# Gated cross-attention with a routed feed-forward: ScalarE issues the copy of the negated maxima itself, in place of SyncE

## What is computed

```python
def _L0_xattn_ref(q, k, v, mask, Wq, bq, Wk, bk, Wv, bv):
    Qh = (q @ Wq + bq).reshape(B, S, H, dh)      # H = 16 heads, dh = 16
    Kh = (k @ Wk + bk).reshape(B, S, H, dh)
    Vh = (v @ Wv + bv).reshape(B, S, H, dh)
    scores = jnp.einsum('bqhd,bkhd->bhqk', Qh, Kh) / jnp.sqrt(jnp.float32(10.0))
    scores = jnp.where(mask[:, None, None, :] == 0, jnp.float32(-1000000000.0), scores)
    probs = jax.nn.softmax(scores, axis=-1)
    return jnp.einsum('bhqk,bkhd->bqhd', probs, Vh).reshape(B, S, D)
...
x = x + jnp.tanh(g_xattn[0]) * _L0_xattn_ref(_layernorm(x), ctx_1024, ctx_1024, mask, ...)
x = x + jnp.tanh(g_ffn[0]) * _L0_ffn_ref(_layernorm(x), ...)   # 8 experts, each takes its top 1024 tokens
```

## Time and profile before

| | us |
|---|---|
| time before, median of 3 | 867.7 |
| the profiled execution: its own time | 866.8 |
| its span | 865.1 |
| PE busy | 757.8 |
| DVE busy | 556.9 |
| ACT busy | 512.0 |
| mean granted clock of TensorE, share of full | 0.947 |

### The profile page before, as it was taken

How to read it: one execution, slowest core, us unless ns; L and a number is a source line. 1 busy time by engine, 2 the same in 40 slices (tenths; PEclk the granted TensorE clock), 3 DMA queues, 4 the chain that set the end, 5 groups by cost and what they waited for, 6 DMA issues and landing times. The chain is left out here.

```text
span 865.1 us, 24848 instructions
## 1 busy us (share of the span) xinstructions
PE 757.8 (88%) x9570; PEld 634.3 (73%) x9570; DVE 556.9 (64%) x1421; ACT 512.0 (59%) x1004; POOL 375.3 (43%) x793
## 2 busy tenths in 40 slices
PE   1699999999999999999998721599999999999993
PEld 1577788878887888878886510379888888888983
DVE  4367777787777777777767549754746556474440
ACT  3235577766766677767756637265555655556641
POOL 6231444534354344424422430436474654747505
PEclk9889999999999999999999955599999999999997
DMA  4423342444434452444322242135354453624314
GB/s 133 136 89 127 131 156 98 152 157 163 146 122 151 154 178 88 160 162 164 103 102 72 83 138 83 48 126 118 99 104 117 81 113 73 130 45 85 38 13 49
DMA packets 76772, 97.06 MB, mean 112 GB/s; under 512 B 8264, under 2 KB 55880, under 8 KB 76616
## 3 DMA queue, kind: packets, MB, share of 16 engines
q1 hardware_dynamic: 64368, 78.44, 26.7%
q0 software_dynamic: 12288, 17.05, 12.0%
HBM read 52.37 MB, written 25.72 MB: 90 GB/s over the span
## 5 line engine op out<-in xcount | busy, mean ns | idle before, releaser
L676 DVE TENSOR_REDUCE m_sb<-a_ps 128x4 f32<-128x512 f32 x256 | 164.5, 684 | 70.7 <-PE a_ps L905 60.1
L538 ACT ACTIVATE p_t<-b_ps 128x512 f32<-128x512 f32 x256 | 143.6, 588 | 61.1 <-PE b_ps L913 60.9
L905 PE MATMUL a_ps<-k_st,q_st 31*128 31x128 f32 x2048 | 151.0, 285 | 21.6 <-ACT p_t L538 11.4
L905 PEld LDWEIGHTS a_ps<-k_st,q_st 31*128 31x128 f32 x2048 | 127.2, 188 | 47.7 <-issue 37.0
L913 PE MATMUL b_ps<-q_st,k_st 32*128 32x128 f32 x2048 | 149.1, 283 | 1.2 <-ACT p_t L538 1.0
L1223 POOL DMA_INDIRECT out<-y,idx_add x64 | 100.3, 1567 | 110.8 <-ACT y L1282 100.0
L458 POOL TENSOR_TENSOR x<-o_n,x_res 128x256 f32<-128x256 f32 x64 | 47.0, 734 | 194.9 <-DVE o_n L761 171.6
L913 PEld LDWEIGHTS b_ps<-q_st,k_st 32*128 32x128 f32 x2048 | 124.5, 186 | 2.2 <-issue 1.4
L1592 PE MATMUL bank<-x_hi,w_hi 128*128 128x512 f32 x254 | 100.1, 394 | 0.0
L1592 PE MATMUL bank<-x_lo,w_hi 128*128 128x512 f32 x254 | 99.0, 390 | 0.0
L1592 PE MATMUL bank<-x_hi,w_lo 128*128 128x512 f32 x254 | 98.9, 389 | 0.0
(11 more groups left out here) (238 smaller groups left out, 1713.9 us busy)
## 6 DMA issues: line engine op xcount, KB each, us to landing
w<-in_w_t SPq DMA_DIRECT2D x24, 512.0 KB, 4.8
rows_scratch<-xg SPq DMA_DIRECT2D x16, 528.0 KB, 3.0
x_in<-in_x SPq DMA_DIRECT2D x16, 512.0 KB, 4.9
c_t<-in_ctx_t SPq DMA_DIRECT2D x16, 512.0 KB, 5.8
k_st<-k_val SPq DMA_DIRECT2D x64, 128.0 KB
q_st<-q_val SPq DMA_DIRECT2D x64, 128.0 KB, 2.1
x_res<-in_x SPq DMA_DIRECT2D x16, 512.0 KB, 3.8
out<-x SPq DMA_DIRECT2D x16, 512.0 KB, 6.4
```

What stands on the lines that cost most here:

```text
L538: act.activation(p_t[b.s % 2][:, 4 * r:4 * r + 4, :], b_ps[q % 2][:].rearrange("p (h s) -> p h s", s=P), ACT.Exp, scale=SCALE).then_inc(ex ...
L676: dve.tensor_reduce(m_sb[b.s % 2][:, 4 * q:4 * q + 4], a_ps[q % 2][:].rearrange("p (h s) -> p h s", s=P), AX_X, ALU.max).then_inc(max_done, 1)
L905: mm = pe.matmul(a_ps[i][:, t * P:(t + 1) * P], q_st[p][r:r + A_K, t, tok], k_st[p][r:r + A_K, t, tok], start=True, stop=True)
```

## The change

The function max_rows moves from SyncE's program to ScalarE's. It keeps its wait (for neg_done of the same batch, now on the engine that signals it), its source, its destination and its semaphore. On SyncE it stood in every step ahead of stack_k and stack_q; on ScalarE it stands behind exp 1 and ahead of xn_t_out, q_out and pv_copy. It goes out on ScalarE's own DMA queue, which the kernel before doesn't use.

```diff
@@ SyncE
-            def max_rows(b):
-                if b.ok:
-                    sp.wait_ge(neg_done, b.times(1, 1))
-                    sp.dma_start(q_st[b.group.p][MAX_ROW:P:RG, :, b.j * P:(b.j + 1) * P], neg_m[b.s % 2][:]).then_inc(s_m[b.s % 2], 16)
...
                 if b.j == 3:
                     store_rows(g.on(-3))
-                max_rows(b.back(1))
                 if b.j == 1:
                     stack_k(g.on(1))
@@ ScalarE
+            def max_rows(b):
+                if b.ok:
+                    act.wait_ge(neg_done, b.times(1, 1))
+                    act.dma_start(q_st[b.group.p][MAX_ROW:P:RG, :, b.j * P:(b.j + 1) * P], neg_m[b.s % 2][:]).then_inc(s_m[b.s % 2], 16)
...
                 exp(b.back(2), 0)
                 negate(b.back(1))
                 exp(b.back(2), 1)
+                max_rows(b.back(1))
                 if b.j == 0:
```

## The result

The changed kernel takes 885.6 us (median of four runs, 883.1 to 888.7) against 867.6 before (four runs, 866.6 to 867.8): 1.021 times as long, 95% interval 1.019 to 1.023. I had forecast 867.9 with a range of 863.5 to 873.2. It is 18 us slower, and the time lies well outside the range. All ratios in this document leave out slow executions, of which there is one: of the eleven of experiment e5 one took 3140.6 us.

A forecast was written before the change was run, and what follows sets the result against it. TensorE was taken to bound the attention stage. A gain of 3.9 us at j = 1, less 3.8 at j = 0 and 0.3 in the last steps, gave +0.2 us: 867.9 us, range 863.5 to 873.2.

The forecast's parts named there:

- the gap ahead of the scores at j = 1: PE idle ahead of scores x = 0, waiting for neg_m's copy behind loads; falls to 0.17 us, gaining 3.9 us.
- The issue on ScalarE: Between exp 1 and what follows: overlaps exp 1, delays xn_t_out by 0.34 us at j = 0; 3.8 us in all there.
- VectorE's idle time ahead of xn_lo: Sign at j = 0: grows from 0.52 to about 0.86 us because xn_hi is late.
- the gap ahead of L876: Sign at j = 0: PE is idle some 0.2 us there.
- j = 1 and 3 are hidden: After the issue comes pv_copy, which waits 1.39 us for TensorE anyway, so the delay costs nothing.
- at j = 2: q_out 0.34 us late; 0.18 absorbed in pv_copy's wait, exp 2 and 3 shift by 0.16, hidden from PE.
- The first rival: The issue doesn't hold ScalarE up, so only the gain of 3.9 us is left: 863.8 us; chance 0.25.
- the second: The issue doesn't overlap exp 1, or is as much longer: 6.3 us more at j = 0, 874.2 us; chance 0.17.
- The third: SyncE's stack_q and ScalarE's issue at j = 2 shut each other out: 4.8 us more, 872.7 us; chance 0.08.
- the sentence on SyncE: SyncE, freed of 64 issues and the neg_done wait, sends the x2 store and stack_q up to 1.5 us sooner; costed nothing.
- the landing: neg_m's copy on its own queue lands 2.8 us after issue, at 210.0; worst end: when it does now.
- The fourth rival: The own queue brings nothing and the copy lands when it does now: 1.3 us lost, 869.0 us; chance 0.10.

The follow-up runs named there:

- e5: Kernel before the change, but at j = 0 SyncE issues the copy of neg_m ahead of the four loads; 863.3 us, 0.9945 of before.
- e6: Changed kernel, but at j = 0 SyncE waits for ScalarE's copy to land before issuing loads and store; 863.9 us, 0.9965 of before.
- e7: As e6, but at j = 0 ScalarE issues the copy behind xn_t_out instead of ahead of it; 863.1 us, 0.9943 of before.
- e1: Changed kernel, but SyncE holds the store of x2 until xn_hi is rounded, so it goes out behind the copy; 868.8 us, 1.0015 of before.
- e2: Kernel before the change, but SyncE issues the store of x2 at j = 0, ahead of the copy; 898.6 us, 1.032 of before.
- e4: Kernel before the change, but GpSimd issues the copy at j = 0 on its software queue; 901.0 us, 1.037 of before.

## Why the prediction was wrong

**What held.** TensorE bounds the stage, and the gap ahead of the scores at j = 1 was the copy's landing, though the profile named VectorE: e5 shows it, and its worth, 4.0 us of gaps where 3.9 were summed. The issue on ScalarE overlaps exp 1 and holds back what follows: it takes 0.54 us (0.59 assumed), starts 0.03 us after negate's end, and xn_hi starts 0.62 us after that end, 0.23 later than before (0.34 forecast). VectorE's idle time ahead of xn_lo is 0.79, forecast 0.86, and the gap ahead of L876 0.24, forecast "some 0.2". As a cost that is 3.4 us by the gaps, 3.6 by the traces of e6 and e7, where 3.8 stood in the sum; the measured times don't settle it. j = 1 and 3 are hidden, and at j = 2 pv_copy's wait shrinks from 0.35 to 0.18 us as worked out, with no PE gap behind it. The first rival (no hold-up on ScalarE) falls by the late xn_hi, the second (issue behind exp 1) by the issue at 214.76, while exp 1 ran until 215.21. The third (issues shut each other out) falls at j = 2 of group 6: the issue at 230.25 took 0.54 us, though SyncE's stack_q issues ran from 229.46 to 232.71.

**The step that failed** is the sentence on SyncE: the store of x2 "goes out up to 1.5 us sooner ... I cost this at nothing". I asked only whether anyone waits for the store. The question left out was whom the store gets in front of. The copy's place on SyncE's queue was doing work: its wait for neg_done kept the 0.5 MB store back until the copy was out. With that wait gone the store goes out first, and the gaps, which were to shrink by 3.9 us, grow by 12.2. e1, which puts back that order alone, has all of it back: its gaps are 4.5 us, where they were 6.3 before the change.

**The bounds failed with it.** For the landing I took the best case (2.8 us, from the gathers of the second stage) and called "when it does now" the worst end. But that end supposed the same traffic ahead of the copy. The fourth rival had the queue nearly right (its own queue brings nothing) and gave 869.0; e1, with the store in its old place, measures 868.8. With the store ahead it would have come to about 885: 1.4 us more in each of twelve groups, in whose gaps the 0.26 then hides whole, and 0.9 for the other groups and the last steps, on 867.7. Measured, each of the twelve groups is some 1.3 us longer (1.0 in the gap at j = 1, 0.24 ahead of L876). That the two agree has some luck in it: only 0.34 MB more than before came ahead of the copy's last packet, 0.9 us at 370 GB/s, and the slower traffic (340 GB/s beside the copy, where it was 372) did the rest. The row of the gathers was also the wrong neighbour: nothing in it says what had been issued before them.

**The rules of the Trainium skill.** The round-robin over queues ("DMA: Bandwidth & Descriptors", "Queues, rings and completion order") did not let the copy pass here: 20 packets of an otherwise empty queue moved only after 1.27 MB of another. The trace shows when packets move and not when the queue had them, so it doesn't tell whether the rule itself fails; once they move, they do so beside the store's. The other sentence of that page, in "Issuing engines are not separate DMA queues", that the DMAs of all issuing engines run on the same DMA engines and interleave, is the one that the measurement agrees with. Its case, the own queue bringing nothing, was in the prediction with a chance of 0.10, and that isn't exact either: beside e2 the own queue made each gap 0.75 us shorter.

## What to carry to other kernels

Before moving a DMA to another engine's queue, write down the order of all issues in time, before and after, with their bytes: a small copy that someone waits for can have to wait for what was issued before it on another queue (here for 2.0 to 2.3 of 2.4 MB), and a wait that is taken off an engine lets what stood behind it go first. If the trace shows an idle gap whose named releaser was done long before, look for a small DMA behind large ones and put the small one first; here that was one moved line, for 0.55%, where moving the issue to another engine cost 2.1%.

## What the runs showed of the hardware

A queue of its own doesn't put a small copy ahead of traffic on another queue. A copy of 8 KB, issued while 1.2 to 1.7 MB of SyncE's queue were still to move, moved no packet for 3.0 to 4.2 us after its issue in group 6, on ScalarE's hardware queue (e1, the changed kernel) and on GpSimd's software queue (e4, 3.9 us). It did pass a store issued 1.2 us after it (e1), and the last 0.1 to 0.3 MB of one issued up to 0.9 us before it (the changed kernel). What makes that order these runs don't tell.

After some of the long gaps TensorE's clock falls too. Stretches of e2 behind a gap of 2.65 us that ended at 193.80 (columns as in the earlier trace rows):

```profile
193.00:194.00 1.00, 0.17 (x4) 0.20 (x8) 0.00 (x0) 0.00 (x0) 0.70 (x4) 1.00 0.07 14
194.00:195.00 1.00, 1.00 (x28) 1.00 (x31) 0.00 (x0) 0.00 (x0) 0.68 (x4) 0.61 0.02 6
195.00:196.00 1.00, 1.00 (x14) 0.78 (x11) 0.45 (x1) 0.34 (x1) 0.23 (x1) 0.50 0.00 0
...
198.00:199.00 1.00, 1.00 (x33) 0.81 (x32) 0.75 (x1) 0.00 (x0) 0.00 (x0) 1.00 0.00 0
```

The granted clock falls to 0.50, the lower of the two levels (1.2 GHz), at 194.2 and is back at 1.00 3.4 us later. From 100 to 440 us that happened five times in e2 (one of them lasted 6.8 us) and not once in the changed kernel, whose gaps from 100 us on are at most 2.15 us. The length of the gap alone doesn't decide it: in e2 the falls came with gaps of 2.04, 2.06, 2.45, 2.65 and 2.94 us, and none came with those of 2.37 and 2.74. The rows of the two kernels, e2 first:

```profile
100.00:440.00 340.00, 308.04 (x5355) 255.52 (x5354) 237.19 (x606) 217.85 (x450) 133.49 (x433) 0.97 0.40 134
```

```profile
100.00:440.00 340.00, 316.39 (x5645) 262.62 (x5641) 249.88 (x643) 232.12 (x477) 141.78 (x455) 1.00 0.41 139
```

(1 - 0.97) x 340 is 10 us, about the 10.8 us that e2's gaps leave unexplained. So the same fault cost half as much again on top of the gaps themselves once they grew from 1.5 to 2.3 us on average.
